# Experts of layer 0: the first product with the weights stationary, copied per tile by VectorE

## Chip, core and metric

One NeuronCore of a Trainium2 chip runs the whole program. Time is device time of one execution in microseconds (us); the profile is one further execution, seen by the hardware profiler. TensorE multiplies, VectorE (DVE) and ScalarE (ACT) work element by element, GpSimd (POOL) issues the DMAs that gather and scatter rows, SyncE (SP) issues all others.

## The reference

The program is a graph network of two layers on 6250 nodes of 256 features; each layer sums an attention over edges, a mixing branch and a mixture of experts. The change lies in the experts of layer 0: a gate picks two of eight experts for a node, and each expert is two products with a ReLU between.

```python
gate_logits = x_flat @ Wg + bg + bias
topk_vals, topk_idx = jax.lax.top_k(gate_logits, TOP_K)          # 2 of 8
h = jax.nn.relu(jnp.einsum('td,edh->teh', x_flat, W1) + b1)       # 256 -> 512
y = jnp.einsum('teh,ehd->ted', h, W2) + b2                        # 512 -> 256
out = jnp.einsum('ted,te->td', y, combine)
```

The kernel computes an expert only for the rows that chose it.

## The kernel before

`stage_route` sorts the 2 x 6250 pairs of row and expert into 108 tiles of 128 slots (`SLOT_TILES`), each tile of one expert, and leaves for each tile the rows to fetch (`slot_row`), the places for its results (`slot_home`) and its expert's number (`tile_expert`). While VectorE does that, SP loads all weights of the eight experts into SBUF (`ExpertInputs.load`, four pieces an expert: `w1s`, `w2s`, and the biases `b1s` and `b2s`, broadcast over the 128 partitions). A barrier ends the stage.

`stage_experts` then goes through the 108 tiles. GpSimd gathers a tile's 128 rows from HBM (`get`, line 1936) and scatters its results (`put`, line 1942). TensorE has four steps for a tile:

- `turn_x` (line 1961): two transposes of 128x128, rows to columns; ScalarE copies the result out of PSUM (`keep_x`).
- `widen` (line 1971): the first product, x of the tile stationary, the expert's 512 columns of W1 moving, in two halves of the 256 features. VectorE adds the bias row out of PSUM (`bias`, line 2024).
- `turn_h` (line 1982): four transposes of h; ScalarE applies the ReLU on the way out of PSUM (`relu`, line 2013).
- `narrow` (line 1992): the second product, four parts of 128, turned h stationary, W2 moving. VectorE adds its bias (`keep_y`, line 2033).

The order is written out by hand: `all_turns` runs each engine's steps for different tiles in one pass, so that while TensorE does `narrow` of tile j it has done `turn_h` of j + 1, `widen` of j + 2 and `turn_x` of j + 3. The loop turns 25 times over four tiles, with the first and the last four written out. Semaphores count tiles; each engine's sequencer takes its instructions in order, so a wait holds up all that follows on its engine. The expert's number is read from SBUF into registers (`expert_of`, line 1926) to form the address of the weights; this happens on TensorE for `widen` and `narrow`, on VectorE for `bias` and `keep_y`. Buffers: `xin`, `y` four deep, `xt`, `h`, `ht` and all PSUM tiles two deep.

Of the kernel before, what the change touches and what calls it, by code (L numbers as in the profile page):

```python
# [12 lines left out]
ALU = mybir.AluOpType  # L13
ACT = mybir.ActivationFunctionType
AX = mybir.AxisListType
ds = bass.ds

P = 128
# [18 lines left out]
D = 256  # L37
# [1395 lines left out]
EXPERTS = 8  # L1433
# [27 lines left out]

SLOT_TILES = -(-((2 * N + EXPERTS * (P - 1)) // P) // 4) * 4
WIDE_E = 512
HOT_RING = 4


class ExpertInputs:


    def __init__(self, nc, own, w1, b1, w2, b2):  # L1470
        def sb(name, shape):
            return own.enter_context(nc.sbuf_tensor(name, shape, F32))
        self.w1s, self.w2s = sb("w1s", [P, EXPERTS * 2, WIDE_E]), sb("w2s", [P, EXPERTS * 4, D])
        self.b1s, self.b2s = sb("b1s", [P, EXPERTS, WIDE_E]), sb("b2s", [P, EXPERTS, D])
        self.of = w1, b1, w2, b2
        self.weights_in = own.enter_context(semaphore(nc, "expert_weights_in"))

# [2 lines left out]
    def load(self, sp, piece):  # L1480
        w1, b1, w2, b2 = self.of
        e = piece // 4
        to, of = ((self.w1s[:, e * 2:e * 2 + 2, :], w1[e].rearrange("(c p) n -> p c n", p=P)),
                  (self.w2s[:, e * 4:e * 4 + 4, :], w2[e].rearrange("(c p) n -> p c n", p=P)),
                  (self.b1s[:, e, :], b1[e:e + 1, :].to_broadcast([P, WIDE_E])),
                  (self.b2s[:, e, :], b2[e:e + 1, :].to_broadcast([P, D])))[piece % 4]
        sp.dma_start(to, of).then_inc(self.weights_in, 16)

# [229 lines left out]
def stage_route(nc, g, comb, inputs):  # L1718
# [4 lines left out]
    with stage(nc) as own:  # L1723
# [9 lines left out]
        at = sb("at8", [P, NTP])  # L1733
# [30 lines left out]
        with nc.Block() as block:  # L1764
            @block.sync
            def _(sp):
                for piece in range(inputs.PIECES):
                    inputs.load(sp, piece)

            @block.gpsimd  # L1770
            def _(pool):
# [26 lines left out]
            def _(dve):  # L1798
# [54 lines left out]
                for t in range(2 * NT):  # L1853
                    i, k = t // 2, t % 2
                    if t >= HOT_RING:
                        dve.wait_ge(placed, t - (HOT_RING - 1))
# [22 lines left out]
def stage_experts(nc, g, inputs, xn_rows, y_rows):  # L1879


    RING, AHEAD = 4, 6
    TURNS = SLOT_TILES // RING
    PE_, DVE_ = mybir.EngineType.PE, mybir.EngineType.DVE
    with stage(nc) as own:
        def sb(name, shape, dt=F32):
            return own.enter_context(nc.sbuf_tensor(name, shape, dt))

        def sem(name):
            return own.enter_context(semaphore(nc, name))  # L1890

        def pb(name):
            return own.enter_context(nc.psum_tensor(name, [P, 2, 512], F32))
        xin = sb("xin_e", [P, RING, D])
        xt = sb("xt_e", [P, 2, 2, P])
        h = sb("h_e", [P, 2, WIDE_E])
        ht = sb("ht_e", [P, 2, 4, P])
        y = sb("y_e", [P, RING, D])
        ps_x, ps_h, ps_ht, ps_y = pb("ps_xe"), pb("ps_he"), pb("ps_hte"), pb("ps_ye")
        loaded = [sem(f"x_in{r}") for r in range(RING)]  # L1900
        out = [sem(f"y_out{r}") for r in range(RING)]
        x_turned, x_kept, h_made, h_ready = sem("x_turned_e"), sem("x_kept_e"), sem("h_made_e"), sem("h_ready_e")
        h_turned, ht_ready, y_made, y_kept = sem("h_turned_e"), sem("ht_ready_e"), sem("y_made_e"), sem("y_kept_e")

        def later(turn, r, by):
            return turn + (r + by) // RING, (r + by) % RING
# [18 lines left out]
        def expert_of(i, engine):  # L1925
            _, values = nc.values_load_multi_w_load_instructions(g.tile_expert[0:1, ds(i, 1)], engines=(engine,),
                                                                 min_val=0, max_val=EXPERTS - 1)
            return values[0]
        with nc.Block() as block:
# [23 lines left out]
            @block.tensor  # L1953
            def _(pe):
                def turn_x(turn, r, new, first):
                    j = turn * RING + r
                    pe.wait_ge(loaded[r], turn * 16 + 16)
                    if not new:
                        pe.wait_ge(x_kept, j - 1)
                    for c in range(2):  # L1960
                        last = nc.tensor.transpose(ps_x[:, r % 2, c * P:(c + 1) * P], xin[:, r, c * P:(c + 1) * P], g.ident[:, :])
                    last.then_inc(x_turned, 1)

                def widen(turn, r, new, first):
                    j = turn * RING + r
                    e = expert_of(j, PE_)
                    pe.wait_ge(x_kept, j + 1)
                    if not new:
                        pe.wait_ge(h_ready, j - 1)
                    for c in range(2):  # L1970
                        last = nc.tensor.matmul(ps_h[:, r % 2, :], xt[:, r % 2, c, :],
                                                inputs.w1s[:, :, :].rearrange("p a n -> p (a n)")[:, ds(e * (2 * WIDE_E) + c * WIDE_E, WIDE_E)],
                                                start=(c == 0), stop=(c == 1))
                    last.then_inc(h_made, 1)

                def turn_h(turn, r, new, first):
                    j = turn * RING + r
                    pe.wait_ge(h_ready, j + 1)
                    if not new:
                        pe.wait_ge(ht_ready, j - 1)  # L1980
                    for c in range(4):
                        last = nc.tensor.transpose(ps_ht[:, r % 2, c * P:(c + 1) * P], h[:, r % 2, c * P:(c + 1) * P], g.ident[:, :])
                    last.then_inc(h_turned, 1)

                def narrow(turn, r, new, first):
                    j = turn * RING + r
                    e = expert_of(j, PE_)
                    pe.wait_ge(ht_ready, j + 1)
                    if not new:
                        pe.wait_ge(y_kept, j - 1)  # L1990
                    for c in range(4):
                        last = nc.tensor.matmul(ps_y[:, r % 2, 0:D], ht[:, r % 2, c, :],
                                                inputs.w2s[:, :, :].rearrange("p a n -> p (a n)")[:, ds(e * (4 * D) + c * D, D)],
                                                start=(c == 0), stop=(c == 3))
                    last.then_inc(y_made, 1)
                pe.wait_ge(inputs.weights_in, 16 * inputs.PIECES)
                all_turns(pe, [(3, turn_x), (2, widen), (1, turn_h), (0, narrow)])

            @block.scalar
            def _(act):  # L2000
                def keep_x(turn, r, new, first):
                    j = turn * RING + r
                    act.wait_ge(x_turned, j + 1)
                    if not new:
                        act.wait_ge(h_made, j - 1)
                    nc.scalar.copy(xt[:, r % 2, :, :].rearrange("p c n -> p (c n)"), ps_x[:, r % 2, 0:D]).then_inc(x_kept, 1)

                def relu(turn, r, new, first):
                    j = turn * RING + r
                    act.wait_ge(h_turned, j + 1)  # L2010
                    if not new:
                        act.wait_ge(y_made, j - 1)
                    nc.scalar.activation(ht[:, r % 2, :, :].rearrange("p c n -> p (c n)"), ps_ht[:, r % 2, :], ACT.Relu).then_inc(ht_ready, 1)
                all_turns(act, [(3, keep_x), (1, relu)])

            @block.vector
            def _(dve):
                def bias(turn, r, new, first):
                    j = turn * RING + r
                    e = expert_of(j, DVE_)  # L2020
                    dve.wait_ge(h_made, j + 1)
                    if not new:
                        dve.wait_ge(h_turned, j - 1)
                    nc.vector.tensor_tensor(h[:, r % 2, :], ps_h[:, r % 2, :],
                                            inputs.b1s[:, :, :].rearrange("p a n -> p (a n)")[:, ds(e * WIDE_E, WIDE_E)], ALU.add).then_inc(h_ready, 1)

                def keep_y(turn, r, new, first):
                    j = turn * RING + r
                    e = expert_of(j, DVE_)
                    dve.wait_ge(y_made, j + 1)  # L2030
                    if not first:
                        dve.wait_ge(out[r], turn * 16)
                    nc.vector.tensor_tensor(y[:, r, :], ps_y[:, r % 2, 0:D],  # L2033
                                            inputs.b2s[:, :, :].rearrange("p a n -> p (a n)")[:, ds(e * D, D)], ALU.add).then_inc(y_kept, 1)
                dve.wait_ge(inputs.weights_in, 16 * inputs.PIECES)
                all_turns(dve, [(2, bias), (0, keep_y)])


class TableWeights:
# [1136 lines left out]
```

## Time and profile before

| | us |
|---|---|
| median of 3 runs | 6626.58 |
| lowest, highest | 6622.57, 6632.74 |
| the profiled execution | 6622.28 |
| its span in the trace | 6620.4 |

Busy shares of the span: PE 75%, PEld (TensorE's weight loads, which overlap PE) 53%, DVE 66%, ACT 27%, POOL 52%. They are means over some twenty stages; the experts of layer 0 take the stretch from about 2755 to 3210 us. The last chain of waits of the page lies in another stage, the one that ends the program, and says nothing of this one. Matmuls are pipelined and their ends are modelled, so that a step is read from start to start.

### The profile page before, as it was taken

The page shows a single profiled execution, that of the slowest core. Times are in us where ns is not written, and L with a number is a line of the kernel's source. Part 1 is how long each engine was busy: PE and PEld are TensorE (multiplying, and loading weights), DVE is VectorE, ACT ScalarE, POOL GpSimd, SP SyncE. Part 2 cuts the span into 40 slices and gives each one's busy share as a digit, 9 for nine tenths or more (in the row PEclk, how much of TensorE's full clock was granted, in tenths as well). Part 3 has the DMA queues.
Part 4 walks back from the last instruction along what each step waited for, and adds up shares of the span by engine and source line. Part 5 has one row for each costly group of instructions (what it writes and reads, how often), then busy time and mean ns, then how long its engine had stood idle before and what let it go on. Part 6 is the DMA issues. An engine that isn't in the chain of part 4 may idle for free. (4 is left out here: it accounts for less than half of the span.)

```text
span 6620.4 us, 90044 instructions
## 1 busy us (share of the span) xinstructions
PE 4933.3 (75%) x21196; PEld 3530.4 (53%) x21197; DVE 4377.2 (66%) x8953; ACT 1781.3 (27%) x4856; POOL 3455.1 (52%) x3669
## 2 busy tenths in 40 slices
PE   1456666677776764699767677778788877999999
PEld 1345555555555552366544444445555546666665
DVE  8987777888878878622566666666767666333333
ACT  7322232222332223222320000012222215333332
POOL 0117777777777775144147777777777754000000
PEclk9978888888888886799888888887877778999999
DMA  1012222222222222322455555555555533000001
GB/s 59 16 41 58 57 57 57 56 58 57 58 56 58 56 57 68 112 64 63 137 151 140 139 139 139 138 143 147 146 146 148 146 108 84 5 5 10 5 5 39
DMA packets 380678, 534.74 MB, mean 81 GB/s; under 512 B 119263, under 2 KB 240118, under 8 KB 380406
## 3 DMA queue, kind: packets, MB, share of 16 engines
q0 software_dynamic: 139648, 299.92, 19.0%
q1 hardware_dynamic: 240886, 233.29, 11.7%
q8 instruction: 43, 0.70, 0.0%
q14 instruction: 101, 0.83, 0.0%
HBM read 475.96 MB, written 56.96 MB: 80 GB/s over the span
## 5 line engine op out<-in xcount | busy, mean ns | idle before, releaser
L877 POOL DMA_INDIRECT got<-table,st_idx x3232 | 3075.1, 951 | 1012.1 <-issue 910.2
L955 PE MATMUL ps_sum<-weighted,hot 128*128 128x260 f32 x6464 | 1845.1, 443 | 178.0 <-DVE acc L1027 173.2
L955 PEld LDWEIGHTS ps_sum<-weighted,hot 128*128 128x128 f32 x6464 | 1383.2, 225 | 591.5 <-DVE acc L1027 267.5
L1027 DVE TENSOR_TENSOR acc<-acc,ps_sum 128x260 f32 x1664 | 707.1, 425 | 741.1 <-PE ps_sum L955 605.5
L940 PE MATMUL ps_score<-score_split,hot_t 128*128 x3232 | 246.5, 184 | 980.5 <-DVE z L1007 954.4
L1019 DVE TENSOR_TENSOR weighted<-got,ps_weight 128x2048 f32<-128x2048 f32 x404 | 921.5, 2281 | 4.3 <-ACT weighted L915 0.8
L940 PEld LDWEIGHTS ps_score<-score_split,hot_t 128*128 128x128 bf16 x3232 | 191.4, 100 | 1161.7 <-issue 1143.5
L912 ACT ACTIVATE ps_weight<-z 128x32 f32<-128x32 f32 x404 | 81.2, 201 | 2655.7 <-DVE z L1007 2655.7
L3061 DVE SCALAR_TENSOR_TENSOR x_res<-ps_yf,comb,x_res 128x256 f32 x392 | 189.7, 484 | 637.8 <-PE ps_yf L2969 637.8
L978 DVE TENSOR_TENSOR hot<-ps_score,row_loc 128x1024 f32<-128x1024 f32 x404 | 492.0, 1218 | 3.5
L2949 PE MATMUL ps_hf<-acc,ws_f 128*128 (+2 forms) x896 | 348.0, 542 | 6.3 <-ACTq L2996 6.3
L2969 PE MATMUL ps_yf<-ws_f,h2t 128*128 128x256 f32 x1568 | 347.7, 379 | 0.8 <-ACT h2t L3009 0.8
L2949 PE MATMUL ps_hf<-h1t,ws_f 128*128 128x384 f32 (+1 forms) x896 | 346.0, 539 | 0.8 <-ACT h1t L3009 0.8
L2969 PEld LDWEIGHTS ps_yf<-ws_f,h2t 128*128 128x128 f32 x1568 | 297.9, 190 | 53.5 <-ACT h2t L3009 1.4
L996 DVE TENSOR_REDUCE row_score<-ps_score 128x64 f32<-128x192 f32 (+1 forms) x404 | 162.5, 402 | 240.9 <-DMA got<-table,st_idx 240.1
L3009 ACT ACTIVATE h2t<-ps_hf,own_scale 128x512 f32<-128x512 f32 x224 | 162.2, 724 | 508.1 <-PE ps_hf L2949 508.1
L2949 PEld LDWEIGHTS ps_hf<-acc,ws_f 128*128 128x128 f32 x896 | 171.0, 191 | 173.8 <-issue 114.9
L2949 PEld LDWEIGHTS ps_hf<-h1t,ws_f 128*128 128x128 f32 x896 | 170.2, 190 | 155.9 <-issue 107.1
L263 POOL TENSOR_TENSOR shifted<-xs,pivot 128x256 f32<-128x256 f32 x49 | 45.3, 925 | 379.4 <-DVE pivot L401 230.3
L1942 POOL DMA_INDIRECT y_rows<-y_e,slot_home x108 | 106.6, 987 | 209.9 <-DVE y_e L2033 205.3
L3009 ACT ACTIVATE h1t<-ps_hf,own_scale 128x512 f32<-128x512 f32 x224 | 162.1, 724 | 173.4 <-PE ps_hf L2949 173.4
L985 DVE TENSOR_SCALAR hot_t<-spread,lane 128x1024 bf16<-128x1024 bf16 x404 | 201.9, 500 | 7.1 <-DMA spread<-row_list 6.8
(533 smaller groups left out, 7392.6 us busy)
## 6 DMA issues: line engine op xcount, KB each, us to landing
spread<-row_list SPq DMA_DIRECT2D x404, 256.0 KB
got<-table,st_idx POOLq DMA_INDIRECT x3232, 2.7
gate_xin<-ball_rows SPq DMA_DIRECT2D x98, 128.0 KB
got_y_e<-y_rows SPq DMA_DIRECT2D x10, 896.0 KB
table<-row_e SPq DMA_DIRECT2D x50, 130.0 KB, 2.7
ball_rows<-xt SPq DMA_DIRECT2D x10, 640.0 KB, 4.7
mix_xin<-ball_rows SPq DMA_DIRECT2D x49, 128.0 KB
xn_rows<-xs_m SPq DMA_DIRECT2D x49, 128.0 KB, 1.7
```

Source lines behind the costliest of these rows:

```text
L877: pool.indirect_dma_start(got[:, r, k, :], None, table, bass.IndirectOffsetOnAxis(ap=st_idx[:, r, k:k + 1], axis=0))\
L940: last = nc.tensor.matmul(scores[:, k, :], hot_t[:, r % 2, k, :], split[:, :, :, :].rearrange("p t a c -> p (t a c)")[:, ds(b * SP, SP)], ...
L955: last = nc.tensor.matmul(ps_g[:, p % 2, 0:AW], hot[:, r % 2, k, :], weighted[:, r % 2, k, :], start=(k == n * p), stop=(k == n * p + n - 1))
L978: nc.vector.tensor_tensor(hot[:, r % 2, :, :], count_to.unsqueeze(1).to_broadcast([P, KT, P]), g.row_loc[:, ds(i * KT, KT)].unsqueeze(2).t ...
L985: nc.vector.tensor_scalar(hot_t[:, r % 2, :, :].rearrange("p k n -> p (k n)"), spread[:, r % SPREAD_RING, :], g.lane[:, 0:1], None, ALU.is ...
L996: link(nc.vector.tensor_reduce(row_score[:, :, :], scores.rearrange("p k (a c) -> p k c a", a=PARTS), AX.X, ALU.add))
L1019: nc.vector.tensor_tensor(out, v, w, ALU.mult).then_inc(scaled, 1)
L1027: nc.vector.tensor_tensor(acc[:, ds(b * AW, AW)], acc[:, ds(b * AW, AW)], ps_g[:, p % 2, 0:AW], ALU.add).then_inc(added, 1)
L2949: last = nc.tensor.matmul(ps_h[:, j, 0:HALVES[hf][1]], ws[:, par, l, c, f * P:(f + 1) * P], rhs(c, hf), start=(c == 0), stop=(c == 1))
L2969: last = nc.tensor.matmul(ps_y[:, k % 4, 0:D], h2[:, c, k * P:(k + 1) * P], ws[:, par, 2, c, :], start=(c == 0), stop=(c == 1))
L3009: nc.scalar.activation(h[:, f, at:at + n], ps_h[:, j, 0:n], ACT.Relu, bias=own_s[:, par, 1, l, f:f + 1], scale=own_s[:, par, 0, l, f:f + 1])\
L3061: nc.vector.scalar_tensor_tensor(xr, ps_y[:, k % 4, 0:D], comb[:, ds(t * 8 + pair * 2 + par, 1)], xr, ALU.mult, ALU.add).then_inc(y_used, 1)
```

## The change

The first product comes out turned. W1 becomes the stationary operand, in eight blocks of 128x128, and the turned x of the tile moves: out come four blocks of 128 hidden features by 128 slots, which is what `narrow` needs. `turn_h` goes, with its PSUM tile and its VectorE step. The bias now belongs to partitions, so that ScalarE can add it with the ReLU, in four ops, one for each block. Since the stationary operand is to lie at an address that needs no register, VectorE copies the tile's W1 with its bias columns, 1028 columns, into a ring of four (`copy_w1`); the expert's number is read for that copy instead of for `widen`. The bias b1 is loaded by column, four-byte elements, instead of by broadcast.

```diff
+FIRST_E = 2 * WIDE_E + WIDE_E // P
...
-        self.w1s, self.w2s = sb("w1s", [P, EXPERTS * 2, WIDE_E]), sb("w2s", [P, EXPERTS * 4, D])
-        self.b1s, self.b2s = sb("b1s", [P, EXPERTS, WIDE_E]), sb("b2s", [P, EXPERTS, D])
+        self.w1s, self.w2s = sb("w1s", [P, EXPERTS, FIRST_E]), sb("w2s", [P, EXPERTS * 4, D])
+        self.b2s = sb("b2s", [P, EXPERTS, D])
...
-                  (self.b1s[:, e, :], b1[e:e + 1, :].to_broadcast([P, WIDE_E])),
+                  (self.w1s[:, e, 2 * WIDE_E:FIRST_E], b1[e].rearrange("(f p) -> p f", p=P)),
...
                 def widen(turn, r, new, first):
                     j = turn * RING + r
-                    e = expert_of(j, PE_)
+                    pe.wait_ge(w1_copied, j + 1)
                     pe.wait_ge(x_kept, j + 1)
                     if not new:
                         pe.wait_ge(h_ready, j - 1)
-                    for c in range(2):
-                        last = nc.tensor.matmul(ps_h[:, r % 2, :], xt[:, r % 2, c, :],
-                                                inputs.w1s[:, :, :].rearrange("p a n -> p (a n)")[:, ds(e * (2 * WIDE_E) + c * WIDE_E, WIDE_E)],
-                                                start=(c == 0), stop=(c == 1))
+                    for f in range(4):
+                        for c in range(2):
+                            at = c * WIDE_E + f * P
+                            last = nc.tensor.matmul(ps_h[:, r % 2, f * P:(f + 1) * P], w1c[:, r, at:at + P], xt[:, r % 2, c, :],
+                                                    start=(c == 0), stop=(c == 1))
                     last.then_inc(h_made, 1)
-
-                def turn_h(turn, r, new, first):
...
-                    pe.wait_ge(ht_ready, j + 1)
+                    pe.wait_ge(h_ready, j + 1)
...
-                all_turns(pe, [(3, turn_x), (2, widen), (1, turn_h), (0, narrow)])
+                all_turns(pe, [(2, turn_x), (1, widen), (0, narrow)])
...
                 def relu(turn, r, new, first):
                     j = turn * RING + r
-                    act.wait_ge(h_turned, j + 1)
+                    act.wait_ge(h_made, j + 1)
                     if not new:
                         act.wait_ge(y_made, j - 1)
-                    nc.scalar.activation(ht[:, r % 2, :, :].rearrange("p c n -> p (c n)"), ps_ht[:, r % 2, :], ACT.Relu).then_inc(ht_ready, 1)
-                all_turns(act, [(3, keep_x), (1, relu)])
+                    for f in range(4):
+                        last = nc.scalar.activation(ht[:, r % 2, f, :], ps_h[:, r % 2, f * P:(f + 1) * P], ACT.Relu,
+                                                    bias=w1c[:, r, 2 * WIDE_E + f:2 * WIDE_E + f + 1])
+                    last.then_inc(h_ready, 1)
+                all_turns(act, [(2, keep_x), (1, relu)])
...
-                def bias(turn, r, new, first):
+                def copy_w1(turn, r, new, first):
                     j = turn * RING + r
                     e = expert_of(j, DVE_)
...
+                    if not first:
+                        dve.wait_ge(h_ready, j - (RING - 1))
+                    nc.vector.tensor_copy(w1c[:, r, :], inputs.w1s[:, :, :].rearrange("p e n -> p (e n)")[:, ds(e * FIRST_E, FIRST_E)]).then_inc(w1_copied, 1)
...
-                all_turns(dve, [(2, bias), (0, keep_y)])
+                all_turns(dve, [(2, copy_w1), (0, keep_y)])
```

The order of instructions follows from `all_turns`. On TensorE, before, one tile of the loop reads as follows (ISA rows are register instructions, TENSOR_LOAD is the read of the expert's number):

```order
L1961 MATMUL ps_xe<-ident,xin_e 128x128 x2
L1926 ISA
L1926 TENSOR_LOAD tile_expert
L1926 ISA x2
L1967 REGISTER_ALU
L1969 REGISTER_ALU
L1971 ISA
L1971 MATMUL ps_he<-w1s,xt_e 128x512
L1971 ISA
L1971 MATMUL ps_he<-w1s,xt_e 128x512
L1982 MATMUL ps_hte<-ident,h_e 128x128 x4
```

After it come the second read of the expert's number and the four products of `narrow`. With the change the same place, up to the first product of `narrow`, reads:

```order
L1963 MATMUL ps_xe<-ident,xin_e 128x128 x2
L1968 REGISTER_ALU
L1975 MATMUL ps_he<-xt_e,w_of_tile 128x128 x8
L1928 ISA
L1928 TENSOR_LOAD tile_expert
L1928 ISA x2
L1984 REGISTER_ALU
L1986 ISA
L1986 MATMUL ps_ye<-w2s,ht_e 128x256
```

One read of the expert's number and the four transposes are gone, and two products have become eight, each with a weight of its own.

On VectorE the first rows of the loop are with the change (`w_of_tile` is the ring that the diff names `w1_of_tile`):

```order
L1928 TENSOR_LOAD tile_expert
L1928 ISA x2
L2019 REGISTER_ALU
L2020 ISA
L2020 COPY w_of_tile<-w1s 128x1028
L1928 ISA
L1928 TENSOR_LOAD tile_expert
L1928 ISA x2
L2025 REGISTER_ALU
L2027 REGISTER_ALU
L2028 ISA
L2028 TENSOR_TENSOR y_e<-ps_ye,b2s 128x256
```

The copy for tile j + 2 stands where `bias` of tile j + 2 stood, ahead of `keep_y` of tile j; both reads of the expert's number stay.

## Rows read from the trace of the kernel before

**Rows 1.** Stretches of the span: busy time of each engine, granted clock, DMA.

```profile
core 0: us, PE busy (x) PEld busy (x) DVE busy (x) ACT busy (x) POOL busy (x), PEclk, DMA share, GB/s
...
1164.20:1166.60 2.40, 2.40 (x24) 2.40 (x24) 2.37 (x3) 1.05 (x3) 1.85 (x2) 1.00 0.32 90
...
2720.00:2740.00 20.00, 13.42 (x38) 3.85 (x37) 20.00 (x114) 0.00 (x0) 0.00 (x0) 0.50 0.00 0
...
2763.00:2766.00 3.00, 3.00 (x4) 1.45 (x5) 0.00 (x0) 0.00 (x0) 0.94 (x1) 0.50 0.30 87
2766.00:2768.00 2.00, 2.00 (x5) 0.77 (x4) 0.69 (x1) 0.37 (x1) 0.00 (x0) 0.82 0.00 0
...
2773.00:3195.50 422.50, 422.50 (x1855) 292.85 (x1854) 115.03 (x206) 99.81 (x206) 199.77 (x204) 1.00 0.21 63
```

**Rows 2.** Groups of the stage, 2758 to 3210: busy us, mean ns, idle before.

```profile
L1942 POOL DMA_INDIRECT y_rows<-y_e,slot_home x108 | 106.6, 987 | 209.9 <-DVE y_e L2033 205.3 <-issue 4.6
L1936 POOL DMA_INDIRECT xin_e<-xn_rows,slot_row x106 | 102.8, 970 | 32.7 <-issue 31.4 <-PE ps_xe L1961 1.3
L2024 DVE TENSOR_TENSOR h_e<-ps_he,b1s 128x512 f32<-128x512 f32 x108 | 74.7, 692 | 176.5 <-PE ps_he L1971 176.5
L1971 PEld LDWEIGHTS ps_he<-w1s,xt_e 128*128 128x128 f32 x432 | 74.6, 192 | 53.7 <-issue 53.7
```

**Rows 3.** The stage in order of time: start us, length us, engine, line, count, idle.

```profile
2755.45 1.19 POOL L1936 DMA_INDIRECT xin_e<-xn_rows,slot_row  x1 [78.16 <-SPq L1929]
...
2759.74 0.69 PE L1961 MATMUL ps_xe<-ident,xin_e 128*128 128x128 f32 x2 [0.49 <-DMA xin_e<-xn_rows,slot_row]
...
2771.15 1.89 PE L1992 MATMUL ps_ye<-w2s,ht_e 128*128 x8
...
2998.57 0.38 PE L1961 MATMUL ps_xe<-ident,xin_e 128*128 128x128 f32 x2
...
2998.78 1.88 PE L1971 MATMUL ps_he<-w1s,xt_e 128*128 x4
2998.87 0.42 DVE L2033 TENSOR_TENSOR y_e<-ps_ye,b2s 128x256 f32<-128x256 f32 x1 [1.47 <-PE ps_ye L1992]
...
3000.50 0.60 PE L1982 MATMUL ps_hte<-ident,h_e 128*128 128x128 f32 x4
...
3000.94 1.89 PE L1992 MATMUL ps_ye<-w2s,ht_e 128*128 x8
...
3002.67 0.38 PE L1961 MATMUL ps_xe<-ident,xin_e 128*128 128x128 f32 x2
...
3203.95 3.62 PE L1992 MATMUL ps_ye<-w2s,ht_e 128*128 x16
...
3221.37 0.89 SPq L2145 DMA_DIRECT2D got_y_e<-y_rows  x2
```

**Rows 4.** The mixer of layer 0 in order of time: `heads` and ScalarE behind it.

```profile
1163.90 2.75 PEld L1286 LDWEIGHTS ps_mix<-mix_xin,wq 128*128 128x128 f32 x24
1163.94 2.92 PE L1286 MATMUL ps_mix<-mix_xin,wq 128*128 128x128 f32 x24
...
1165.55 1.15 ACT L1355 ACTIVATE mix_ut<-ps_mix,bn_beta,bn_gamma 128x128 f32<-128x128 f32 x3 [2.13 <-PE ps_mix L1286]
```

**Rows 5.** Groups of VectorE by shape, whole span.

```profile
L978 DVE TENSOR_TENSOR hot<-ps_score,row_loc 128x1024 f32<-128x1024 f32 x404 | 492.0, 1218 | 3.5
...
L1063 DVE CAST score_split<-weighted 128x600 bf16<-128x600 f32 x3 | 1.4, 473 | 0.1
```

**Rows 6.** Instructions of line 1926: ns shortest/median/longest, first and last start.

```profile
L1926 DVEq TENSOR_LOAD <-tile_expert x216: 299/304/328, 2754.8 to 3206.0; - x108
```

**Rows 7.** DMA issues: count, KB each, median us to landing.

```profile
bn_gamma<-in_L_mix_bn_gamma_dram SPq DMA_DIRECT2D x1, 3.0 KB, 4.8
```

**Rows 8.** Order of time near 1121 us: VectorE and GpSimd side by side.

```profile
1121.12 0.48 DVE L985 TENSOR_SCALAR hot_t<-spread,lane 128x1024 bf16<-128x1024 bf16 x1
1121.30 1.11 POOL L877 DMA_INDIRECT got<-table,st_idx  x1 [0.30 <-issue]
```

More of the change, by code:

```diff
@@ L1482, in load @@
         e = piece // 4
-        to, of = ((self.w1s[:, e * 2:e * 2 + 2, :], w1[e].rearrange("(c p) n -> p c n", p=P)),
+        to, of = ((self.w1s[:, e, 0:2 * WIDE_E].rearrange("p (c n) -> p c n", n=WIDE_E), w1[e].rearrange("(c p) n -> p c n", p=P)),
                   (self.w2s[:, e * 4:e * 4 + 4, :], w2[e].rearrange("(c p) n -> p c n", p=P)),
-                  (self.b1s[:, e, :], b1[e:e + 1, :].to_broadcast([P, WIDE_E])),
+                  (self.w1s[:, e, 2 * WIDE_E:FIRST_E], b1[e].rearrange("(f p) -> p f", p=P)),
                   (self.b2s[:, e, :], b2[e:e + 1, :].to_broadcast([P, D])))[piece % 4]
@@ L1766, in _ @@
             def _(sp):
-                for piece in range(inputs.PIECES):
-                    inputs.load(sp, piece)
+                with nc.allow_non_contiguous_dma(reason="biases by column"):
+                    for piece in range(inputs.PIECES):
+                        inputs.load(sp, piece)
             @block.gpsimd
@@ L1895, in stage_experts @@
         xt = sb("xt_e", [P, 2, 2, P])
-        h = sb("h_e", [P, 2, WIDE_E])
+        w1c = sb("w1_of_tile", [P, RING, FIRST_E])
         ht = sb("ht_e", [P, 2, 4, P])
         y = sb("y_e", [P, RING, D])
-        ps_x, ps_h, ps_ht, ps_y = pb("ps_xe"), pb("ps_he"), pb("ps_hte"), pb("ps_ye")
+        ps_x, ps_h, ps_y = pb("ps_xe"), pb("ps_he"), pb("ps_ye")
         loaded = [sem(f"x_in{r}") for r in range(RING)]
@@ L1902, in stage_experts @@
         x_turned, x_kept, h_made, h_ready = sem("x_turned_e"), sem("x_kept_e"), sem("h_made_e"), sem("h_ready_e")
-        h_turned, ht_ready, y_made, y_kept = sem("h_turned_e"), sem("ht_ready_e"), sem("y_made_e"), sem("y_kept_e")
+        w1_copied, y_made, y_kept = sem("w1_copied_e"), sem("y_made_e"), sem("y_kept_e")
         def later(turn, r, by):
@@ L1969, in widen @@
                         pe.wait_ge(h_ready, j - 1)
-                    for c in range(2):
-                        last = nc.tensor.matmul(ps_h[:, r % 2, :], xt[:, r % 2, c, :],
-                                                inputs.w1s[:, :, :].rearrange("p a n -> p (a n)")[:, ds(e * (2 * WIDE_E) + c * WIDE_E, WIDE_E)],
-                                                start=(c == 0), stop=(c == 1))
-                    last.then_inc(h_made, 1)
-                def turn_h(turn, r, new, first):
[L1977 to L1983, printed above, removed]
+                    for f in range(4):
[3 more added lines that the diff above has]
+                                                    start=(c == 0), stop=(c == 1))
+                    last.then_inc(h_made, 1)
                 def narrow(turn, r, new, first):
@@ L2009, in relu @@
                     j = turn * RING + r
-                    act.wait_ge(h_turned, j + 1)
+                    act.wait_ge(h_made, j + 1)
                     if not new:
                         act.wait_ge(y_made, j - 1)
-                    nc.scalar.activation(ht[:, r % 2, :, :].rearrange("p c n -> p (c n)"), ps_ht[:, r % 2, :], ACT.Relu).then_inc(ht_ready, 1)
-                all_turns(act, [(3, keep_x), (1, relu)])
+                    for f in range(4):
[3 more added lines that the diff above has]
+                all_turns(act, [(2, keep_x), (1, relu)])
             @block.vector
             def _(dve):
-                def bias(turn, r, new, first):
+                def copy_w1(turn, r, new, first):
                     j = turn * RING + r
                     e = expert_of(j, DVE_)
[L2021 to L2025, printed above, removed]
+                    if not first:
+                        dve.wait_ge(h_ready, j - (RING - 1))
+                    nc.vector.tensor_copy(w1c[:, r, :], inputs.w1s[:, :, :].rearrange("p e n -> p (e n)")[:, ds(e * FIRST_E, FIRST_E)]).then_inc(w1_copied, 1)
                 def keep_y(turn, r, new, first):
```

## Prediction

> **What bounds the kernel now.** I read the stretches first, then the groups of the stage, then its order in time, and only then rows of other stages that resemble what the change adds.
>
> The stretches place the edit: it touches the stage of the experts of layer 0, some 450 us of 6620. From 2773 to 3195 TensorE is busy for the whole stretch at a granted clock of 1.00, its 2.4 GHz level [rows 1]; before 2766 it runs at 0.50, the 1.2 GHz level. The groups of the stage say that the others have little to do: VectorE 0.69 and 0.42 us a tile, GpSimd two DMA issues of 0.99 and 0.97 [rows 2, 3], against a tile's period of 4.10 us. The period is read in time [rows 3], from one `turn_x` start, 2998.57, to the next, 3002.67: `turn_x` 0.21 us, `widen` 1.72 (2998.78 to 3000.50), `turn_h` 0.44 (to 3000.94), `narrow` 1.73. The pieces follow each other without a hole, so what TensorE saves in a tile, the stage saves, as long as nothing else becomes longer than the new period. Nothing of the next stage is under way beside it: its first loads stand at 3221.37 [rows 3].
>
> The same rows frame the sum: the first `narrow` starts at 2771.15 and the last two run for 3.62 us from 3203.95, so 436.4 us from the first to the end [rows 3]. By the pieces: 108 `narrow`, 106 `turn_h`, 105 `widen` and 104 `turn_x` lie there, 186.8 + 46.6 + 180.6 + 21.8 = 435.9 us. The count holds.
>
> **The change part by part.**
>
> *`turn_h` goes.* 106 x 0.44 = 46.6 us within that frame.
>
> *`widen` is turned.* Two products of 512 columns become eight of 128 columns. Each float32 product is two matmul passes (432 rows for 216 products, [rows 2]), so 4 passes a tile of 512 columns become 16 of 128: the same columns, but four times the weight loads. The trace has the same thing elsewhere: the mixer's `heads`, float32 products of 128 columns, a new weight with each [rows 4]. The granted clock is 1.00 there [rows 1]. 24 loads take 2.75 us; one takes 0.19 [rows 2], so their step is (2.75 - 0.19) / 23 = 0.111 us: loads overlap each other and the matmuls. I take 0.112 a pass, a little for rounding. 16 x 0.112 = 1.79 us against 1.72. Bounds: 0.109, the step of the present transposes (0.44 / 4, [rows 3]), and for a widening whose first load shows each time, 1.79 + 0.08: the 24 matmuls take 2.92 us, 0.17 more than their loads, of which at least a part is such a start. I take 1.79, since in the stage a load can run under the transposes ahead of it, as it does now.
>
> The rule that speaks against the edit is in the Trainium skill, "TensorE: Matmul & The Clock Gate", section "Back-to-back issue gap": for streams of load and matmul pairs at 128 columns it gives about 81 ns a matmul where the columns alone would take 56, for bfloat16. Were a float32 pass stretched in that proportion, a pass would take 0.162 us, an estimate. The trace disagrees for this shape [rows 4]; what it would do is in the first rival.
>
> *The new period* is 0.21 + 1.79 + 1.73 = 3.73 us, 0.37 less. In the frame: 108 x 1.73 + 106 x 1.79 + 105 x 0.21 = 186.8 + 189.7 + 22.1 = 398.6, that is **-37.3 us**.
>
> *The pipeline is a step shorter, so it fills sooner.* Now three `turn_x`, three `widen` and two `turn_h` precede the first `narrow`, and the third `turn_x` still has to wait for its rows. After, the first `widen` follows the second `turn_x`, at about 2760.4 (2759.74 + 0.69, [rows 3]). At the lower clock its 16 passes take 16 x 0.224 = 3.6 us, `turn_x` 0.43: 2764.4. If the clock rises when it does now, at about 2766.7 (0.82 is the mean from 2766 to 2768, [rows 1]), the second `widen` ends at 2767.3: 10 passes at the lower clock, 6 at the higher. The first `narrow` starts then, **-3.9 us**; -5.0 if the clock is up after the first widening, -3.2 if not before the first `narrow`.
>
> *VectorE: bias out, copy in.* 0.69 us go; a float32 copy of 1028 columns, SBUF to SBUF, comes. The trace has none of this size. Nearest is a one-input cast of 600 columns, 473 ns, in proportion 0.81 us for 1028 and less if part of it is fixed; above it stands a two-input op on 1024 columns, 1.22, below it the cast's own 0.47 [rows 5]. I take 0.8. VectorE then has 0.9 to 1.65 us of work in a 3.73 us period. What counts is its new place in the chain: `copy_w1` of tile j + 2 stands behind `keep_y` of tile j - 1. From rows: `keep_y` starts 0.3 us after the next `turn_x` start (2998.87 against 2998.57, [rows 3]); then the expert's number is read, 0.3 us for the read alone [rows 6], say 0.8 with checks and addresses; then the copy. It is done 1.9 us into a period, 2.3 if it takes 1.22, and its `widen` begins 3.73 + 0.21 us in. TensorE's new wait is therefore over 1.6 us early; queued behind it are only the expert read and `narrow` of the tile before, which starts 1.8 us later still. The copy's own wait, for the ReLU four tiles earlier, is long satisfied. Cost 0; if the cover were gone, all of the excess would come every tile.
>
> *ScalarE.* One op of 512 columns becomes four of 128 columns with a bias column. Three such ops with two columns of scalars take 1.15 us [rows 4], so four take 1.5. With `keep_x`, at most half as long, 2.3 us of 3.73 at the most. The ReLU of tile j follows `widen` j and has the `narrow` of j - 1, `turn_x` and the next `widen` to finish in, 3.7 us. Cost 0.
>
> *GpSimd* issues the same two DMAs; with 0.30 idle ahead of each [rows 8] 2.56 us a tile, under 3.73.
>
> *Loads.* Eight broadcasts of 256 KB become eight transfers of 512 four-byte elements on SP. From 2720 on no DMA runs [rows 1], and the first gather starts at 2755.45 [rows 3]: 35 us of cover. Nearest row: 3.0 KB, 768 such elements, land in 4.8 us [rows 7]. Eight of them one after the other would be 38 us; even so 3 us would be late at most, and since the broadcasts go and transfers overlap, I take 0.
>
> **Sum**: -37.3 - 3.9 = -41.2. The profiled execution took 6622.28, so 6581.1; the median of the runs, 6626.58, stands 4.3 above it, so **6585 us**.
>
> **The rivals.**
>
> *1. Slower: the weight loads show.* If a pass waits for its load, it costs 0.19 us, 16 passes 3.04, and the stage gains 106 x 1.25 = 132 us on the forecast: 6717. It decides from 0.135 us a pass on, where (1.72 + 0.44) / 16 is reached. For it: TensorE has no spare time, and a load takes longer than a pass. Against: the mixer's 24 in a row [rows 4]. At 0.162 it would give 106 x 16 x 0.05 = 85 us on top, 6670. That is the time by the Trainium skill's rule above; by the trace the chance is small: 0.06.
>
> *2. GpSimd becomes the bound.* A fast VectorE op with all operands in SBUF and a DMA issue get in each other's way: an issue of 0.94 us took 1.11 where a 0.48 us op stood at its start [rows 8]. If both issues of a tile waited for a whole copy, GpSimd's period would be 2.56 + 2 x 0.8 = 4.16, and 106 x 0.43 = 46 us go, a little more than the gain: 6631. Against: there is one copy a tile, and with one such wait it is 3.36. The Trainium skill, "SBUF — State Buffer", section "Who interferes with whom", says that the later of the two is blocked until the other's whole instruction is over; the issue lost 0.17 us, where the op still had 0.30 to run. Chance 0.04.
>
> *3. The edit does not do what it says, or another cover fails* (loads late, the clock falls in the stage, TensorE's queue empties at the new wait): anything from no change up. Chance 0.07, half of it slower.
>
> **How the numbers follow.** The forecast has 0.83. Its own range: 0.109 us a pass (106 x 16 x 0.003 = 5 us less), the fill (-1), runs 4 us under their median: 6575; a first load that shows in every `widen` (106 x 0.08 = 8), the fill (+1), runs 6 above, loads 3 us late: 6603. It holds most of 0.83, so I round out to 6573 and leave the other cases outside. A measurement of this kernel can tell 0.2%, 13 us, from no change. Faster: the forecast and a third of case 3, 0.85; same: rival 2 and the rest of 3 that isn't slower, 0.05; slower: rival 1 and half of 3, 0.10.
>
> **What would show it.** Between two `turn_x` starts 3.73 us, in the 16 passes a step of 0.112, the granted clock 1.00 throughout, TensorE still busy for the whole stretch; the copy about 0.8 us; the first `narrow` near 2767 on the present scale; the stage's end 41 us earlier and the rest of the span unchanged. Wrong: holes on TensorE whose releaser is the copy or the ReLU, passes of 0.135 us or more, issues on GpSimd back to back.

## The result, and the profile after

| | before | after |
|---|---|---|
| median, us | 6624.83 (4 runs, 6622.57 to 6632.74) | 6584.60 (4 runs, 6577.88 to 6587.82) |
| the profiled execution, span | 6622.28, 6620.4 | 6586.9, 6585.0 |
| first gather of the stage to the first load of the next | 465.92 | 423.64 |

The ratio is 0.9936, with a 95% interval of 0.9923 to 0.9949: 40 us faster, as forecast (6585), and the whole range of the runs lies inside the predicted one.

The changed kernel's stage in order of time, at its start, in its middle and at its end (start us, length us, engine, line, operation, count, idle before with its releaser):

```profile
2756.41 1.19 POOL L1938 DMA_INDIRECT xin_e<-xn_rows,slot_row  x1 [78.10 <-SPq L1931]
...
2760.73 0.69 PE L1963 MATMUL ps_xe<-ident,xin_e 128*128 128x128 f32 x2 [0.53 <-DMA xin_e<-xn_rows,slot_row]
...
2761.21 3.62 PE L1975 MATMUL ps_he<-xt_e,w_of_tile 128*128 128x128 f32 x16
...
2765.05 2.13 PE L1975 MATMUL ps_he<-xt_e,w_of_tile 128*128 128x128 f32 x16
...
2767.02 1.25 PE L1986 MATMUL ps_ye<-w2s,ht_e 128*128 x5
...
2992.80 0.38 PE L1963 MATMUL ps_xe<-ident,xin_e 128*128 128x128 f32 x2
...
2993.02 1.95 PE L1975 MATMUL ps_he<-xt_e,w_of_tile 128*128 128x128 f32 x16
2993.20 0.42 DVE L2028 TENSOR_TENSOR y_e<-ps_ye,b2s 128x256 f32<-128x256 f32 x1 [1.89 <-PE ps_ye L1986]
...
2994.06 0.70 DVE L2020 COPY w_of_tile<-w1s 128x1028 f32 x1 [0.43 <-issue]
2994.41 1.21 POOL L1944 DMA_INDIRECT y_rows<-y_e,slot_home  x1 [1.57 <-DVE y_e L2028]
...
2994.80 1.89 PE L1986 MATMUL ps_ye<-w2s,ht_e 128*128 x8
2995.01 1.14 ACT L2008 ACTIVATE ht_e<-ps_he,w_of_tile 128x128 f32<-128x128 f32 x4 [1.42 <-PE ps_he L1975]
...
2996.53 0.38 PE L1963 MATMUL ps_xe<-ident,xin_e 128*128 128x128 f32 x2
...
2996.75 1.50 PE L1975 MATMUL ps_he<-xt_e,w_of_tile 128*128 128x128 f32 x12
...
3162.62 3.62 PE L1986 MATMUL ps_ye<-w2s,ht_e 128*128 x16
...
3180.05 0.88 SPq L2140 DMA_DIRECT2D got_y_e<-y_rows  x2
```

Read from start to start, as in [rows 3]: `turn_x` at 2992.80, `widen` 0.22 us later, `narrow` at 2994.80, the next `turn_x` at 2996.53. The tile takes 3.73 us: 0.22 + 1.78 + 1.73. The third piece stands right behind the second; where the transposes of h were is nothing. The copy of 2994.06 is for the tile whose `widen` starts at 2996.75: it is done 1.99 us before that.

The same in stretches (length, then busy time of PE, PEld, DVE, ACT, POOL with instructions, granted clock, DMA share, GB/s):

```profile
core 0: us, PE busy (x) PEld busy (x) DVE busy (x) ACT busy (x) POOL busy (x), PEclk, DMA share, GB/s
2763.00:2766.00 3.00, 3.00 (x18) 3.00 (x18) 0.00 (x0) 1.13 (x5) 0.91 (x1) 0.60 0.31 87
2766.00:2768.00 2.00, 2.00 (x16) 1.90 (x15) 0.00 (x0) 1.05 (x6) 0.94 (x1) 1.00 0.18 45
2768.00:3166.00 398.00, 398.00 (x2767) 370.60 (x2765) 118.92 (x212) 160.27 (x531) 224.82 (x208) 1.00 0.22 68
```

TensorE is busy for all of the 398 us at the 2.4 GHz level, as it was before [rows 1]; the others have become busier (ACT 160 us, POOL 225) and none is near it. The clock is up by 2766, where it was still at 0.50 before [rows 1].

The groups of the changed stage, 2740 to 3180 (line, engine, operation, count, busy us, mean ns of one, idle before and its releasers):

```profile
L1975 PE MATMUL ps_he<-xt_e,w_of_tile 128*128 128x128 f32 x1728 | 212.5, 277 | 0.0
...
L1944 POOL DMA_INDIRECT y_rows<-y_e,slot_home x108 | 128.4, 1189 | 144.2 <-DVE y_e L2028 139.9 <-issue 4.4
L2008 ACT ACTIVATE ht_e<-ps_he,w_of_tile 128x128 f32<-128x128 f32 x432 | 123.1, 367 | 151.3 <-PE ps_he L1975 151.3
L1938 POOL DMA_INDIRECT xin_e<-xn_rows,slot_row x108 | 105.1, 973 | 112.5 <-SPq L1931 78.1 <-issue 31.7 <-PE ps_xe L1963 2.7
L2020 DVE COPY w_of_tile<-w1s 128x1028 f32 x108 | 75.7, 701 | 60.4 <-issue 58.6 <-PEq L97 1.8
```

TensorE's 1728 passes of the first product have no idle time ahead of them. Against [rows 2], the gather is as long as it was (973 ns, 970 before), while the scatter, `put`, went from 987 to 1189 ns.

**What the times of the other stages do.** The stage is 42.3 us shorter, the span of this profile only 35.4. The rest of the span is 6154.5 us before and 6161.4 after. In the seven runs below, all of them built on the changed kernel, the rest is between 6152.6 and 6164.3 us, with the lowest and the highest in two that differ from it in TensorE's stream alone. It wanders by that much from execution to execution, so that a cost or gain of the change outside its stage of a few us can't be told; none is seen. The medians, 40.2 us apart, lie between the two differences. From here on the length of the stage, from its first gather to the next stage's first load, is what tells runs apart to within a microsecond.

### The profile page after: what moved, and what is told of

It reads as the page before. It is cut to its first block and busy times, and to the rows that moved or that the text cites. A ratio compares the mean times of both kernels' runs of the same rounds, so it can differ in the third digit from the quotient of the medians.

```text
span 6585.0 us, 91321 instructions
## 1 busy us (share of the span) xinstructions
PE 4899.5 (74%) x22060; PEld 3601.8 (55%) x22061; DVE 4371.6 (66%) x8953; ACT 1839.1 (28%) x5180; POOL 3473.7 (53%) x3669
## 5 line engine op out<-in xcount | busy, mean ns | idle before, releaser
L1975 PE MATMUL ps_he<-xt_e,w_of_tile 128*128 128x128 f32 x1728 | 212.5, 277 | 0.0
```

Of the source, the lines that this page charges most:

```text
L1975: last = nc.tensor.matmul(ps_h[:, r % 2, f * P:(f + 1) * P], w1c[:, r, at:at + P], xt[:, r % 2, c, :], start=(c == 0), stop=(c == 1))
```

## The experiments

| run | stage, us | against the changed kernel | median, us | ratio to before |
|---|---|---|---|---|
| before | 465.92 | +42.3 | | |
| the changed kernel | 423.64 | | 6584.60 | 0.9936 (0.9923 to 0.9949) |
| transposes put back | 470.77 | +47.1 | 6634.58 | 1.0017 (1.0007 to 1.0026) |
| passes of 64 columns | 622.44 | +198.8 | 6783.12 | 1.0246 (1.0228 to 1.0263) |
| copy three times | 423.63 | 0.0 | 6583.01 | 0.9940 (0.9923 to 0.9956) |
| copy six times | 605.15 | +181.5 | 6768.69 | 1.0216 (1.0198 to 1.0235) |
| half the first product | 327.10 | -96.5 | 6486.98 | 0.9789 (0.9771 to 0.9806) |
| fixed weights | 423.66 | 0.0 | 6583.22 | 0.9935 (0.9917 to 0.9952) |
| TensorE warmed up | 421.45 | -2.2 | 6580.52 | 0.9930 (0.9912 to 0.9948) |

The theory: TensorE's stream of instructions sets the stage, before and after, and the copy, the ReLU and GpSimd lie beside it. The rivals are other engines, the copy's port and the loads of weights. Each difference below shows the lines that matter; "..." stands for what is left out.

### The transposes put back

```diff
...
+                    for c in range(4):
+                        nc.tensor.transpose(ps_spare[:, r % 2, c * P:(c + 1) * P], g.ident[:, :], g.ident[:, :])
                     for c in range(4):
                         last = nc.tensor.matmul(ps_y[:, r % 2, 0:D], ht[:, r % 2, c, :],
```

> The changed kernel with four 128x128 TensorE transposes a tile put back ahead of the second product; they turn the identity into a PSUM tile that nobody reads, so the result is the same and nobody waits for them. Theory (TensorE bounds the stage and the four transposes it lost were the whole gain per tile): the period of 3.73 us rises by 0.42 to 0.46 us, to about 4.17 us, and the run by 45 to 50 us, to about 6632 us, level with the kernel before. Rival (the gain came from ScalarE's or VectorE's shorter chain between the two products, with TensorE only filling the time): TensorE has slack, the period stays within 3.73 to 3.85 us and the run within 6585 to 6598 us.

Its order of time in the middle of the stage:

```profile
2992.53 0.38 PE L1963 MATMUL ps_xe<-ident,xin_e 128*128 128x128 f32 x2
...
2992.75 1.95 PE L1975 MATMUL ps_he<-xt_e,w_of_tile 128*128 128x128 f32 x16
...
2994.53 0.60 PE L1986 MATMUL ps_spare<-ident 128*128 128x128 f32 x4
...
2994.97 1.89 PE L1988 MATMUL ps_ye<-w2s,ht_e 128*128 x8
...
2996.70 0.38 PE L1963 MATMUL ps_xe<-ident,xin_e 128*128 128x128 f32 x2
```

The period is 4.17 us and the transposes take their 0.44 in it. Nobody reads them, and the stage is 47.1 us longer, 0.436 for each of the 108 tiles: TensorE has no slack in a tile. The run comes out a little above the kernel before, by 0.07 to 0.26%; its stage is 4.85 us longer than before. From the first `narrow` with its transposes to the end it takes 446.4 us (2769.31 to 3215.69) in place of 436.4, above all by a first product of 1.78 us in place of 1.72 in 106 tiles; the fill, shorter by 5.1 us as in the changed kernel, gives half of that back.

### Passes of 64 columns

```diff
-                        for c in range(2):
-                            at = c * WIDE_E + f * P
-                            last = nc.tensor.matmul(ps_h[:, r % 2, f * P:(f + 1) * P], w1c[:, r, at:at + P], xt[:, r % 2, c, :],
+                        for half in range(2):
+                            for c in range(2):
+                                at, to = c * WIDE_E + f * P, f * P + half * 64
+                                last = nc.tensor.matmul(ps_h[:, r % 2, to:to + 64], w1c[:, r, at:at + P], xt[:, r % 2, c, half * 64:half * 64 + 64],
```

> The changed kernel with every pass of the first product split in two of 64 columns, with the weights loaded for each: 32 passes a tile in place of 16, the same columns in all. Theory A (a pass of 128 columns lasts what its 128 columns take, the load of the next weights lies beside it with nothing to spare): 64-column passes are then limited by their loads, at the 0.11 us a pass that 128 columns have now or a little less; the first product takes 3.0 to 3.6 us in place of 1.8, the period 4.9 to 5.5 us, the run 6710 to 6775 us. Rival B (loads lie wholly beside the passes with room for half as much again): 32 passes of 0.056 us, the period stays within 3.73 to 3.9 us and the run within 6585 to 6605 us.

Its order of time:

```profile
2993.67 0.38 PE L1963 MATMUL ps_xe<-ident,xin_e 128*128 128x128 f32 x2
2993.78 3.65 PEld L1976 LDWEIGHTS ps_he<-xt_e,w_of_tile 128*128 128x128 f32 x32
2993.89 3.68 PE L1976 MATMUL ps_he<-xt_e,w_of_tile 128*128 128x64 f32 x32
...
2997.41 1.95 PE L1987 MATMUL ps_ye<-w2s,ht_e 128*128 x8
...
2999.19 0.38 PE L1963 MATMUL ps_xe<-ident,xin_e 128*128 128x128 f32 x2
```

32 passes of 64 columns take 3.52 us (2993.89 to 2997.41), 0.110 each: as much as a pass of 128 (1.78 / 16 = 0.111). Half the columns save nothing. The weight loads stand back to back with a step of (3.65 - 0.19) / 31 = 0.112, which points to the load as what the pass waits for; a pass of 64 columns without a load of its own was not run, so another cost of every float32 pass is not ruled out. A pass of 128 columns stands just where the two limits meet: by its columns it would take 0.108, half of a 256-column pass of `narrow` (1.73 / 16). So the mechanism of rival 1 exists, but at 128 columns it costs about 0.003 us a pass: the loads show with narrower blocks, and hardly with these. The Trainium skill, "TensorE: Matmul & The Clock Gate", section "LDWEIGHTS (loading the stationary operand)", gives a load's time as its columns divided by 1.2, in ns, which makes an estimate of 107 ns for 128 columns. The step of 0.110 us at a granted clock of 1.00 is close to that; the load's own row is longer, 0.19 us, and at 0.50 the step is 0.210 us (below), where the measurement decides.

The median is 8 us above the range that Theory A gave, and the start of the stage is why:

```profile
2761.39 6.93 PE L1976 MATMUL ps_he<-xt_e,w_of_tile 128*128 128x64 f32 x32
2768.11 0.63 PE L1963 MATMUL ps_xe<-ident,xin_e 128*128 128x128 f32 x2
...
2775.26 3.27 PE L1987 MATMUL ps_ye<-w2s,ht_e 128*128 x8
2778.36 0.38 PE L1963 MATMUL ps_xe<-ident,xin_e 128*128 128x128 f32 x2
...
2770.00:2775.00 5.00, 5.00 (x25) 5.00 (x25) 0.00 (x0) 0.00 (x0) 0.44 (x1) 0.50 0.09 26
2775.00:2778.00 3.00, 3.00 (x10) 2.46 (x10) 0.00 (x0) 1.14 (x4) 0.00 (x0) 0.51 0.00 0
```

The period of 5.52 us, 1.787 more in each of 106 tiles, makes 189.4 of the 198.8 us and would have left the run at 6774. The other 9.4 come before: TensorE is busy without a hole from 2761.39 on, yet the clock stays at 0.50 until about 2777.9, where in the changed kernel it was up by 2765.4. So the first `narrow` starts 18.67 us behind the first gather (at 2756.59) in place of 10.61, and takes 3.10 us in place of 1.73. Why the clock stays down so long is not shown.

### The copy three and six times

```diff
...
                     nc.vector.tensor_copy(w1c[:, r, :], inputs.w1s[:, :, :].rearrange("p e n -> p (e n)")[:, ds(e * FIRST_E, FIRST_E)]).then_inc(w1_copied, 1)
+                    for again in range(2):
+                        dve.wait_ge(copied_again, 2 * j + again + 1)
+                        nc.vector.tensor_copy(spare[:, :], inputs.w1s[:, again, :]).then_inc(copied_again, 1)
```

with 5 in place of 2 for the second; the tile `spare` and one first step of the semaphore are left out here.

> The changed kernel with VectorE's copy of a tile's weights done two more times, into a tile that nobody reads. Theory (VectorE's part of a tile is 0.70 + 0.42 us and some 0.35 us of issue in 3.73 us; two more copies at 0.7 to 0.85 us bring it to 2.9 to 3.2 us, and a GpSimd instruction loses at most 0.25 us to a copy beside it): hidden, period 3.73 us within 0.05, the run within 6578 to 6600 us; GpSimd's put or get lengthen to 1.2 to 1.4 us. Rival (GpSimd waits out each whole copy, so that 2.16 us of issues, 2.1 us of copies and 0.4 us of reads of its registers make a period of about 4.66 us): +0.93 us a tile, the run at about 6685 us.

The groups of the stage with three copies:

```profile
L2025 DVE COPY spare_e<-w1s 128x1028 f32<-128x1028 f32 x216 | 154.9, 717 | 3.7
L1946 POOL DMA_INDIRECT y_rows<-y_e,slot_home x108 | 128.4, 1189 | 138.3 <-DVE y_e L2033 134.0 <-issue 4.3
L1940 POOL DMA_INDIRECT xin_e<-xn_rows,slot_row x108 | 111.4, 1032 | 112.1 <-SPq L1933 78.1 <-issue 32.3 <-PE ps_xe L1965 1.7
```

155 us of work more on VectorE, and the stage is 423.63 us, unchanged. GpSimd's issues lengthen less than was expected (1.2 to 1.4 us): the gather goes from 973 to 1032 ns, the scatter stays at 1189 (the longest of them, 1405 ns, is 0.42 us above the 987 ns without a copy, where the expectation allowed 0.25), far from what waiting out whole copies would give.

> The changed kernel with VectorE's copy of a tile's weights done five more times, into a tile that nobody reads: one step further than with two more, where the run did not change. Theory (VectorE bounds the stage from the point at which its own work passes 3.73 us): 0.70 + 0.42 us, five copies at 0.72 to 0.80 us and some 0.35 to 0.5 us of issue make a period of 5.1 to 5.6 us, +1.4 to +1.9 us over 106 tiles, the run at 6730 to 6785 us; TensorE then waits for VectorE's addition. Rival (the copies never matter because they run two tiles ahead): the run stays at about 6585 us.

Its order of time:

```profile
2989.98 3.63 DVE L2025 COPY spare_e<-w1s 128x1028 f32<-128x1028 f32 x5
...
2991.23 1.04 POOL L1940 DMA_INDIRECT xin_e<-xn_rows,slot_row  x1 [0.30 <-issue]
...
2993.84 0.42 DVE L2033 TENSOR_TENSOR y_e<-ps_ye,b2s 128x256 f32<-128x256 f32 x1 [0.23 <-issue]
...
2994.80 0.70 DVE L2022 COPY w_of_tile<-w1s 128x1028 f32 x1 [0.54 <-issue]
...
2995.41 3.63 DVE L2025 COPY spare_e<-w1s 128x1028 f32<-128x1028 f32 x5
...
2995.55 2.05 PE L1977 MATMUL ps_he<-xt_e,w_of_tile 128*128 128x128 f32 x16 [1.43 <-DVE w_of_tile L2022]
```

Now VectorE pauses for its own issue alone, and `widen` waits 1.43 us for its weights: the period is 5.43 us here (2990.12 to 2995.55; 5.30 to 5.82, in the mean 5.50), the stage 181.5 us longer. This is how a missing cover looks, and where it ends, by an estimate: the period less the five copies (5.43 - 3.63) leaves 1.80 us for the rest of VectorE's tile, so that 3.73 us have room for two more copies of 0.73, not for three. One detail of the expectation was wrong: it named VectorE's addition as what TensorE would wait for, and it is the copy. The gather of 2991.23 lies wholly beside copies, five of them one behind the other from 2989.98 to 2993.61, and takes 1.04 us where it takes 0.97 without.

### Half of the first product

```diff
-                        for c in range(2):
-                            at = c * WIDE_E + f * P
-                            last = nc.tensor.matmul(ps_h[:, r % 2, f * P:(f + 1) * P], w1c[:, r, at:at + P], xt[:, r % 2, c, :],
-                                                    start=(c == 0), stop=(c == 1))
+                        at = f * P
+                        last = nc.tensor.matmul(ps_h[:, r % 2, f * P:(f + 1) * P], w1c[:, r, at:at + P], xt[:, r % 2, 0, :],
+                                                start=True, stop=True)
```

> The changed kernel without the second half of the features in the first product (8 passes a tile in place of 16), so that its result leaves out that half of each sum. Theory (TensorE bounds the stage alone, and GpSimd's 2.56 us a tile, the next in line, is still shorter): the period falls by 8 passes of 0.112 us, from 3.73 to 2.80 to 2.90 us, and the run by 88 to 98 us, to 6487 to 6500 us. Rival (GpSimd or the transfers are next at once: put, get and their issue stretched by the copies, or the 256 KB a tile): a period of 3.0 us or more, the run at 6508 us or above, with TensorE waiting for a gathered tile or for the buffer of a result.

Its order of time, and GpSimd's scatter among the groups of its stage:

```profile
2991.54 0.38 PE L1963 MATMUL ps_xe<-ident,xin_e 128*128 128x128 f32 x2
...
2991.76 1.06 PE L1974 MATMUL ps_he<-xt_e,w_of_tile 128*128 128x128 f32 x8
...
2994.38 0.38 PE L1963 MATMUL ps_xe<-ident,xin_e 128*128 128x128 f32 x2
```

```profile
L1944 POOL DMA_INDIRECT y_rows<-y_e,slot_home x108 | 124.9, 1156 | 52.1 <-issue 36.0 <-DVE y_e L2027 16.1
```

The period is 2.84 us, 0.89 less, eight passes of 0.111; the median, 6486.98, stands at the lower end of what was expected. TensorE bounds the stage here too, with no idle time ahead of its products, so the change had all the room that it used and 0.89 us more. Not much beyond that: the scatter's idle time is now mostly the 0.30 of issue, so that GpSimd takes 1.16 + 0.98 + 2 x 0.30 = 2.74 us a tile, 0.1 from being the bound.

### Fixed weights

```diff
...
-        w1c = sb("w1_of_tile", [P, RING, FIRST_E])
+        w1c = sb("b1_of_tile", [P, RING, WIDE_E // P])
...
-                            last = nc.tensor.matmul(ps_h[:, r % 2, f * P:(f + 1) * P], w1c[:, r, at:at + P], xt[:, r % 2, c, :],
+                            last = nc.tensor.matmul(ps_h[:, r % 2, f * P:(f + 1) * P], inputs.w1s[:, 0, at:at + P], xt[:, r % 2, c, :],
```

VectorE's copy shrinks to the four bias columns, 0.17 us. There is no time for the other way to do without the copy, a product that reads the tile's own W1 by the expert's number from a register; these fixed weights stand in for it.

> The changed kernel without the copy of the 1024 weights a tile: the first product of every tile reads the weights of expert 0 where they lie (so that its result is that of another expert's weights), and VectorE copies only the four bias columns. Theory (the copy is hidden with over 1.6 us to spare, and its only trace is GpSimd's put at 1.19 us in place of 0.99 us): the period stays within 3.68 to 3.78 us, the run within 6575 to 6597 us, the put goes back to 0.97 to 1.05 us. Rival (the copy costs time on the path, by the shared port or by a late start of the first product): the period falls to 3.5 to 3.65 us, the run to 6558 to 6575 us.

The groups of its stage that answer to the copy and the scatter:

```profile
L1944 POOL DMA_INDIRECT y_rows<-y_e,slot_home x108 | 106.5, 986 | 166.3 <-DVE y_e L2028 161.7 <-issue 4.6
```

Without the copy the scatter is back at 986 ns (987 before, [rows 2]) and the stage takes 423.66 us against 423.64. So the copy is what lengthens the scatter, by 0.20 us, and neither the copy nor the longer scatter costs the stage anything.

### TensorE warmed up

```diff
...
+                for k in range(16):
+                    nc.tensor.transpose(ps_spare[:, k // 4 % 2, k % 4 * P:(k % 4 + 1) * P], g.ident[:, :], g.ident[:, :])
                 all_turns(pe, [(2, turn_x), (1, widen), (0, narrow)])
```

> The changed kernel with 16 TensorE transposes of the identity, into a PSUM tile that nobody reads, while the stage's first gathers are under way. Theory (the granted clock is 0.50 at the start of the stage because TensorE did little before it, and work without use raises it as well as work of use): the first product of the stage runs at the full clock, 1.8 to 2.1 us in place of 3.62 us, and the first narrow passes come 1.5 to 2.0 us sooner behind the first get than the 10.6 us of the changed kernel; the run gains about as much, 1.5 to 2.0 us, too little to tell by times alone. Rival (the clock rises with the work of the stage alone, or falls again before the first tile has landed): the first product still takes 3.6 us and nothing moves.

Its order of time at the stage's start:

```profile
2758.02 3.65 PE L1992 MATMUL ps_spare<-ident 128*128 128x128 f32 x16 [4.01 <-PEq L97]
2758.68 1.19 POOL L1938 DMA_INDIRECT xin_e<-xn_rows,slot_row  x1 [78.12 <-SPq L1931]
...
2763.32 1.95 PE L1975 MATMUL ps_he<-xt_e,w_of_tile 128*128 128x128 f32 x16
...
2767.11 1.89 PE L1986 MATMUL ps_ye<-w2s,ht_e 128*128 x8
```

The first product takes 1.95 us, the first `narrow` comes 8.43 us after the first gather (2758.68 to 2767.11) and not 10.61, and the stage is 2.2 us shorter, a little more than expected, since the two `turn_x` around the first `widen` and the second `widen` gain by the higher clock too. Work without use raises the clock as well as work of use: the granted clock is up at about 2762.5, 3.8 us behind the first gather, where in the five runs with the same opening but without this work it was up 7.5 to 9.1 us behind it. This version is ahead of both kernels in the stage; in whole times 2 us are below what can be measured, and its ratio does not differ from that of the changed kernel.

## Why the prediction was right, term by term

| term | predicted | measured |
|---|---|---|
| period of a tile | 3.73 us | 3.73 us |
| first `narrow` to the end | 436.4 to 398.6 + 0.5: -37.3 | 2767.02 to 3166.24, 399.2: -37.2 |
| first gather to the first `narrow` | -3.9 | 15.70 to 10.61: -5.1 |
| sum | -41.2 | -42.3 (the stage), -40.2 (medians) |
| the copy, and its lead | 0.8 us, over 1.6 us early | 0.70 us, 1.99 us early |
| four ReLUs | 1.5 us | 1.14 us |
| GpSimd a tile | 2.56 us | 1.19 + 0.97 + 2 x 0.30 = 2.76 us |

The *first three steps* held as they stood: `turn_h` goes whole (the transposes put back cost 0.44 us a tile again), a pass takes 0.111 us in the stage as in the mixer [rows 4], and TensorE's pieces follow each other without a hole. That the mixer's rows could be carried over fits with the passes of 64 columns: a pass has the step of its load, and the load is of the same size in both places.

The *fill* is the term that was mis-sized, by 1.2 us, and 0.9 of that lies in the second `widen`. The clock rose soon after that `widen` began, at about 2765.4, not after most of it: 2765.05 to 2767.02 is 1.97 us where 2.9 were reckoned. The lower clock gave 0.213 us a pass (2761.21 to `turn_x` at 2764.62, 3.41 us for 16), not 0.224. I had left the rise where it stood before, at 2766.7 [rows 1], though TensorE's first work differs now; the bound of -5.0 that the prediction names for "up after the first widening" was the right case. What sets the moment of the rise is not shown. In five runs whose TensorE does the same until the first `narrow`, it came 7.5 us (six copies) to 9.1 us behind the first gather, so that the second `widen` ended 9.92 to 10.63 us behind it: the fill is worth 5.1 to 5.8 us. The warmed-up run shows from the other side what the lower clock costs here. (The prediction also counts three `turn_x` ahead of the first `narrow` before the change. There are four, as its own 104 behind it says; no number hangs on it.)

*Luck* has a part in the last digits. The median of 6584.60 against a forecast of 6585 is closer than the runs allow, which lie between 6577.88 and 6587.82; the stage gained 42.3 us where 41.2 were reckoned, and the rest of the span, which wanders by more than that, brought the medians to 40.2.

*ScalarE and VectorE* were both over-priced, from rows of other forms, and nothing hung on either. The copy's lead came out by two errors that nearly cancel: the sum left out the addition itself, 0.42 us, and took 0.8 us for the read behind it, which took 0.43. *GpSimd* was under-priced: rival 2's mechanism exists. The copy lengthens a scatter that stands beside it by 0.20 us in the mean, and its longest in the stretch from 2770 to 3150 is 1.40 us for 0.99. What the rival had wrong is the size: it let an issue wait for the whole copy, twice a tile. The Trainium skill, "SBUF — State Buffer", section "Who interferes with whom", says that of a VectorE op in a mode that takes both port pairs and a GpSimd op, the later one is fully blocked for the other's whole instruction. Whether this copy runs in such a mode no run here shows; if it does, the measurement decides otherwise for these issues: a scatter loses at most 0.42 us, and a gather wholly beside five copies loses 0.07 us (1.04 for 0.97), where a full block would have held it until a copy ended, and three copies a tile moved nothing in the stage. *The loads* of the bias stayed hidden: 2.0 KB landed in 6.1 us in the median, the last issue standing at 2704.2, 52 us ahead of the first gather.

## What to carry to other kernels

Where one engine is busy without a hole through a stage, count its pieces from start to start and take out what an edit takes out; put new work on engines whose busy time is far below the period, and price the point at which the cover ends (here two more copies) rather than the copy itself. A product can be turned by swapping its operands, so that no transpose follows; it costs more weight loads, and these are free only while the columns of a pass take as long as its load. Here, in float32, that is so at 128 columns with nothing to spare (0.111 us a pass, 0.108 by the columns alone), and at 64 columns it is not (0.110 us).

## What the runs showed of the hardware beyond that

- A float32 pass of 64 columns takes as long as one of 128, 0.110 and 0.111 us, when each has a weight load of its own.
- A float32 copy of 1028 columns from SBUF to SBUF takes 0.70 us, less than a cast of 600 columns to bfloat16 in proportion (0.81, [rows 5]).
- At a granted clock of 0.50 the step is nearly double: 0.213 us for passes of 128 columns, 0.210 for passes of 64 (2761.39 to 2768.11, 6.72 us for 32). With 64 columns as long as 128 there too, the load's step follows the granted clock.
- Sixteen transposes of no use, made while TensorE would have waited for its first rows, bring the first product from 3.62 to 1.95 us.
- With passes of 64 columns TensorE was busy without a hole, and the clock stayed at 0.50 for 21.3 us from the first gather on, in place of 9.0 (one profile each; the cause is not shown).
